# The late count read within the next uses, and the selection, ranks, masks and statistics of a neighbour-maximum kernel put at other uses

## The reference

```python
h = jnp.maximum(_layernorm(x, axis=-1), 0.0)
mask = A != 0                                   # A is adj
scores = jnp.where(mask, -jnp.arange(N), -inf)
vals, idx = jax.lax.top_k(scores, 25)           # the first 25 neighbours
feats = where(valid, h[idx], -inf); agg = feats.max(axis=2)
agg = jnp.where(degree <= 25, jnp.maximum(agg, 0.0), agg)
out = relu(concat([h, agg]) @ W + b)
return x + out
```

## Time and profile before

| what | us |
|---|---|
| median of 3 runs | 750.21 (750.12 to 751.39) |
| profiled execution | 756.99 |
| its span on the core | 755.3 |
| PE busy | 607.5 |
| DVE busy | 612.1 |
| ACT busy | 425.0 |
| POOL busy | 49.6 |
| mean granted TensorE clock | 0.966 of full |

### The profile page before, as it was taken

The page is one execution under the profiler, slowest core; times in us unless marked ns, Lnnn a source line. Parts: engine busy times, 40 slices in busy tenths (PEclk is TensorE's granted clock), DMA queues, the critical chain, the costliest instruction groups (busy, mean ns, idle before and its releaser), DMA issues.

```text
span 755.3 us, 9644 instructions
## 1 busy us (share of the span) xinstructions
PE 607.5 (80%) x2689; PEld 243.3 (32%) x2720; DVE 612.1 (81%) x813; ACT 425.0 (56%) x579; POOL 49.6 (7%) x38
## 2 busy tenths in 40 slices
PE   0555499888989799888889798898888699897975
PEld 0111133333333333334333333343333333342322
DVE  6111398987989789897989788997989498998986
ACT  0366374866367482686568483767569373746210
POOL 3000000300003000110003000210002000210000
PEclk9997699999999999999999989999999899999999
DMA  9584443547544663538744563548544662230100
GB/s 302 191 250 158 122 162 85 213 124 245 161 167 146 144 248 77 187 140 236 214 160 151 136 249 90 192 144 269 167 174 146 200 220 54 88 122 29 56 15 14
DMA packets 107877, 117.94 MB, mean 156 GB/s; under 512 B 74435, under 2 KB 94150, under 8 KB 103366
## 3 DMA queue, kind: packets, MB, share of 16 engines
q1 hardware_dynamic: 107846, 117.61, 49.1%
HBM read 58.85 MB, written 20.97 MB: 106 GB/s over the span
## 4 chain that ended last, share of the span: by engine, by line
PE 34%; DVE 24%; issue 15%; ACT 11%; SPq 10%; DMA 5%; DVEq 1%; ACTq 0%; another core or an unknown queue 0%
PE picked L556 10%; DVE best L729 9%; PE picked L557 9%; DVE late_hot L735 5%; PE ring L505 4%; SPq L239 4%; ACT late_rank L401 3%; DVE hot L710 3%; PE side L517 3%; SPq L241 3%; PE side L516 3%; SPq L263 3%; DMA mask_t<-mask 3%; DVE best L828 3%; ACT late L413 2%
## 5 line engine op out<-in xcount | busy, mean ns | idle before, releaser
L729 DVE TENSOR_TENSOR best<-picked,best 128x1024 f32<-128x1024 f32 x224 | 268.2, 1217 | 43.4 <-PE picked L557 42.3
L556 PE MATMUL picked<-hot,h_hi 128*128 128x512 f16 x512 | 201.4, 393 | 42.4 <-DVE best L729 28.9
L557 PE MATMUL picked<-hot,h_lo 128*128 128x512 f16 x512 | 199.9, 390 | 0.0
L408 ACT ACTIVATE chosen<-side,bias_cut 128x512 bf16<-128x512 f32 x128 | 88.0, 687 | 117.5 <-PE side L517 107.0
L556 PE MATMUL picked<-late_hot,hi_skew 128*128 128x512 f16 x336 | 127.6, 380 | 12.5 <-DVE late_hot L735 8.5
L557 PE MATMUL picked<-late_hot,lo_skew 128*128 128x512 f16 x336 | 127.3, 379 | 0.0
L828 DVE TENSOR_TENSOR best<-picked,best 128x1024 f32<-128x1024 f32 x84 | 102.6, 1221 | 8.2 <-PE picked L557 8.2
L401 ACT ACTIVATE late_rank<-ring,late_bias 128x512 bf16<-128x512 f32 x128 | 81.7, 688 | 44.3 <-PE ring L505 40.9
L710 DVE TENSOR_SCALAR hot<-rank 128x4096 f16<-128x4096 bf16 x64 | 83.3, 1303 | 26.7 <-ACT rank L401 26.7
L556 PEld LDWEIGHTS picked<-hot,h_hi 128*128 128x128 f16 x512 | 50.9, 99 | 153.5 <-DVE best L729 73.5
L437 ACT COPY best<-picked 128x1024 f32<-128x1024 f32 x32 | 32.3, 1014 | 113.5 <-PE picked L557 113.5
(11 more groups left out here) (72 smaller groups left out, 381.2 us busy)
## 6 DMA issues: line engine op xcount, KB each, us to landing
adj_in<-in_adj_dram SPq DMA_DIRECT2D x15, 2048.0 KB, 7.9
kept<-chosen SPq DMA_DIRECT2D x128, 128.0 KB, 1.8
picks<-kept SPq DMA_DIRECT2D x16, 1024.0 KB, 4.7
late_skew<-late SPq DMA_DIRECT2D x32, 192.0 KB, 2.3
x_in<-in_x_dram SPq DMA_DIRECT2D x8, 512.0 KB, 8.5
xres<-in_x_dram SPq DMA_DIRECT2D x16, 256.0 KB, 7.8
late_skew<-late SPq DMA_DIRECT2D x16, 256.0 KB, 2.4
late_skew<-late SPq DMA_DIRECT2D x32, 128.0 KB, 2.1
```

The costliest lines, as they stand in the source:

```text
L408: nc.scalar.activation(chosen[:, k, :], side[:, :], ACT.Sign, bias=bias_cut[:, 0:1], scale=-1.0).then_inc(chosen_made, 1)
L556: nc.tensor.matmul(dst, hi[:, slot, k, :], onehot, start=start, stop=False)
L557: return nc.tensor.matmul(dst, lo[:, slot, k, :], onehot, start=False, stop=stop)
L729: nc.vector.tensor_tensor(best[:, half, s, :, :], picked[s][:, :, :], best[:, half, s, :, :], ALU.max).then_inc(picked_read, 1)
```

## The change

- DVE: `count_rounds` moves from the end of a step (after `finish_group`) into the next step, behind the take of use 4 (COUNT_USE).
- PE and ACT: of the 8 late ranks 6 (LATE_EARLY) stay at a step's end, late ranks 6 and 7 move to use 4 of the next step (LATE_REST_USE). Late rank 3 on PE comes behind pick 3 instead of ahead of it. Ring positions are renumbered.
- Selection at uses 6 to 13 instead of 4 to 11, ranks at 5 to 11 instead of 4 to 11 (two at use 5); within a use the rank comes first.
- ACT: the four mask quarters at uses 5, 8, 10, 12 instead of after the uses; the waits for the transposes of the masks before and for adj stand ahead of the first quarter. find_late in one piece after the uses instead of at 12 and 14.
- Statistics at uses 13 and 14 and moments at 15 of the even step instead of 4, 5, 6 of the odd one; the spread at the even step's end; the gain at use 5 instead of 8.
- SP: the load of adj for g + 4 at a step's start; xres for g + 2 at its end.
- PE keeps the number that it waits for in a register (`known_due`).

```diff
-    SELECT_WITH, RANK_WITH = spread_over(4, 11), spread_over(4, 11)
-    FLAG_USES, RELU_USE, LATE_HOT_USES = (12, 14), 13, (7, 9)
-    STATS_USES, MOMENTS_USE, SPREAD_USE, GAIN_USE = (4, 5), 6, 7, 8
+    SELECT_WITH, RANK_WITH = spread_over(6, 13), spread_over(5, 11)
+    LATE_EARLY, LATE_REST_USE, COUNT_USE, LATE_HOT_USES = 6, 4, 4, (7, 9)
+    MASK_USES, RELU_USE = (5, 8, 10, 12), 13
+    STATS_USES, MOMENTS_USE, GAIN_USE = (13, 14), 15, 5
...
-    RANK_AT, LATE_AT = 0, K
+    FIRST_RING = K + LATE_EARLY
+    REST_AT, RANK_AT, LATE_AT = -LATE_EARLY, K - LATE_EARLY, 2 * K - LATE_EARLY
```

On SP, in a step:

```diff
-                if not at_end(it, u, 1):
-                    sp.wait_ge(result_made, g + 1)
-                    load_xres(g + 1, (u + 1) % 2)
+                if not at_end(it, u, 4):
+                    load_adj(g + 4, u % 2)
...
                 sp.wait_ge(stored[u % 2], 16 * (it * (UNROLL // 2) + u // 2 + 1))
-                if not at_end(it, u, 4):
-                    load_adj(g + 4, u % 2)
+                if not at_end(it, u, 2):
+                    load_xres(g + 2, u % 2)
```

On ACT:

```diff
                 for use in range(PAIRS, USES):
+                    if use == LATE_REST_USE:
+                        for k in range(LATE_EARLY, K):
+                            stage(at + REST_AT, k, late_rank, late_bias[:, k:k + 1])
+                    for k in RANK_WITH[use] if more else []:
+                        stage(at + RANK_AT, k, rank[:, (u + 1) % 2], late_bias[:, 0:1])
                     for k in SELECT_WITH[use] if not at_end(it, u, 2) else []:
                         choose(g + 2, k)
-                    for k in RANK_WITH[use] if more else []:
-                        stage(at + RANK_AT, k, rank[:, (u + 1) % 2], late_bias[:, 0:1])
-                    if use == SPREAD_USE and new_batch:
-                        spreads(batch)
+                    if use in MASK_USES and not at_end(it, u, 3):
+                        make_masks((u + 1) % 2, [MASK_USES.index(use)])
                     if use == RELU_USE and new_batch:
                         relu_parts(batch, slot)
-                    if use in FLAG_USES and more:
-                        for p in range(2):
-                            p += 2 * FLAG_USES.index(use)
-                            find_late(p, (u + 1) % 2, at + RANK_AT + 2 * p + 2)
+                if more:
+                    for p in range(PAIRS):
+                        find_late(p, (u + 1) % 2, at + RANK_AT + 2 * p + 2)
                 if new_batch:
                     turned_h(batch, slot)
-                if not at_end(it, u, 3):
-                    make_masks((u + 1) % 2)
+                if u % PER_BATCH == 0 and not at_end(it, u, PER_BATCH):
+                    spreads(batch_of(it, u) + 1)
...
-                    for k in range(K):
+                    for k in range(LATE_EARLY):
                         stage(at + LATE_AT, k, late_rank, late_bias[:, k:k + 1])
```

On PE:

```diff
                     pick_pair(g, use, slot)
+                    if use == LATE_REST_USE:
+                        for k in range(LATE_EARLY, K):
+                            late_ranks(g, at + REST_AT, k)
+                    for k in RANK_WITH[use] if more else []:
+                        ranks(g + 1, at + RANK_AT, k)
                     for k in SELECT_WITH[use] if not at_end(it, u, 2) else []:
                         place(g + 2, k, (CHAINS + 1) * g + 1)
-                    for k in RANK_WITH[use] if more else []:
-                        ranks(g + 1, at + RANK_AT, k)
...
                     late_ranks(g + 1, at + LATE_AT, 2)
+                    pick_pair(g + 1, 3, next_slot)
                     late_ranks(g + 1, at + LATE_AT, 3)
-                    pick_pair(g + 1, 3, next_slot)
                 project(g, it, u, new_batch)
                 if more:
-                    for k in range(HALF, K):
+                    for k in range(4, LATE_EARLY):
                         late_ranks(g + 1, at + LATE_AT, k)
```

On DVE:

```diff
                     take_pair(g, use, s)
                     if use == 5:
                         make_hot(BASE, s)
+                    if use == COUNT_USE:
+                        count_rounds(g, s)
                     if use in LATE_HOT_USES:
-                        dve.wait_ge(ring_read, at)
+                        dve.wait_ge(ring_read, at + REST_AT + K)
                         make_late_hot(LATE_HOT_USES.index(use), numbers[:, 1:2])
-                    if use in STATS_USES and new_batch:
+                    if use in STATS_USES and ahead:
...
                 finish_group(g, s, 16 * (it * (UNROLL // 2) + u // 2 + 1))
-                if more:
-                    count_rounds(g + 1, 1 - s)
```

More of the change, by code:

```diff
@@ L220, in ring_of @@
         def ring_of(it, u):
-            return (it * UNROLL + u + 1) * RING
+            return (it * UNROLL + u) * RING + FIRST_RING
         @block.sync
@@ L393, in make_masks @@
                 act.wait_ge(adj_loaded[slot], adj_due[slot])
-                for q in range(Q):
+            def make_masks(slot, quarters):
+                if 0 in quarters:
+                    await_masks(slot)
+                for q in quarters:
                     counts = adj_in[:, slot, q * N:(q + 1) * N].bitcast(U32)
@@ L445, in _ @@
                 choose(0, k)
-            make_masks(1)
+            make_masks(1, range(Q))
             turned_h(0, 0)
@@ L449, in _ @@
             for k in range(K):
-                stage(RANK_AT, k, rank[:, 0], late_bias[:, 0:1])
+                stage(0, k, rank[:, 0], late_bias[:, 0:1])
             find_late(0, 0, K)
@@ L457, in _ @@
                 choose(1, k)
[L458 to L460 removed]
+            for k in range(LATE_EARLY):
+                stage(K, k, late_rank, late_bias[:, k:k + 1])
+            make_masks(0, range(Q))
             def step(it, u):
@@ L600, in _ @@
             for k in range(K):
-                ranks(0, RANK_AT, k)
+                ranks(0, 0, k)
             pe.wait_ge(lo_made, 1)
@@ L607, in _ @@
                 place(1, k, None)
-            for k in range(K):
-                late_ranks(0, LATE_AT, k)
+            for k in range(LATE_EARLY):
+                late_ranks(0, K, k)
             pe.wait_ge(chosen_made, 2 * K)
@@ L800, in step @@
                 batch = batch_of(it, u + 1)
+                ahead = u % PER_BATCH == 0 and not at_end(it, u, PER_BATCH)
                 for use in range(PAIRS, USES):
@@ L806, in step @@
                         make_hot(BASE, s)
+                    if use == COUNT_USE:
+                        count_rounds(g, s)
                     if use in LATE_HOT_USES:
-                        dve.wait_ge(ring_read, at)
+                        dve.wait_ge(ring_read, at + REST_AT + K)
                         make_late_hot(LATE_HOT_USES.index(use), numbers[:, 1:2])
-                    if use in STATS_USES and new_batch:
+                    if use in STATS_USES and ahead:
                         half = STATS_USES.index(use)
-                        stats_of(batch, range(half * HALF, (half + 1) * HALF))
-                    if use == MOMENTS_USE and new_batch:
-                        moments_of(batch)
+                        stats_of(batch_of(it, u) + 1, range(half * HALF, (half + 1) * HALF))
+                    if use == MOMENTS_USE and ahead:
+                        moments_of(batch_of(it, u) + 1)
                     if use == GAIN_USE and new_batch:
```

9 lines of the change are left out of this document (6 added, 3 removed).

## The result

The change makes the kernel slower: **767.97 us** median of four runs (765.04 to 769.08) against 750.80 of four runs of the kernel before beside it (750.12 to 754.99), a ratio of **1.0211, interval 1.0163 to 1.0258**.

The account below looks back on a forecast made before the run. DVE (81%) and PE (80%) were taken as nearly full, leaving DVE's idle time and longer instructions; step changes, tails of -2.2 and clock +3 summed to +16.8 us on 756.99, scaled to 750.2 + 16.6 = 767, range 742 to 777.

Parts of the forecast that it names:

- Part 1: Count at use 4: 2.2 us less in 15 tails, count's 1.52 now in the front, true gain 0.7 a step.
- Part 2: Statistics a step sooner: some 2.1 us leave odd fronts and enter even ones, sum zero for a full DVE.
- Part 3: Gain at use 5: late_hot of use 7 waits for POOL's second instruction, 2.6 us; 1.2 more, 0.9 on the path.
- Part 4: ACT's new order: odd fronts +2.85 us, masks land 5.3 behind take 4, even front 24.95; the dear one.
- the six takes named: DVE's takes 7, 8, 9, 11, 12, 13 in even fronts, stalling on ACT's pace, together 4.1 us.
- Masks in time: Faster rival: masks land before 4.6 us behind take 4, even fronts 22.5, odd 21.7, total 730, halfway 740; chance 0.25.
- Part 5: PE's idle of 2.5 us in even fronts lowers its clock: 1.0 us in steps 2, 6, 10, each between 0 and 2.2.

Follow-up runs that it names:

- both_gain_late: Changed kernel with SP's mask transposes ahead of h's skew, all ACT mask quarters behind the uses, and the gain at use 9: 736.03 us, 0.9776.
- count_swap: flags_after with SP issuing the mask transposes ahead of the skew of h: 734.81 us, 0.9756.
- gain_late: Changed kernel with the gain at use 9 instead of 5: 758.09 us, 1.0077.
- count_and_uses: Changed kernel's count and later selection and ranks, with statistics, gain, find_late and masks as in the kernel before: 751.10 us, 0.9973.
- flags_after: count_and_uses with all find_late behind the uses, as in the change: 747.90 us, 0.9911.
- count_swap_sel: count_swap with selection at uses 5 to 12 and ranks at 4 to 11, each shifted one use sooner: 726.04 us, 0.9652.
- masks_first: Changed kernel with SP issuing the four mask transposes ahead of the skews of h: 756.48 us, 1.0058.
- quarters_after: Changed kernel with all four ACT mask quarters back behind the uses: 755.08 us, 1.0040.

## Why the prediction was right, and where it was off

The forecast was 767 us, with a range of 742 to 777 and slower at 0.70; the result is 768. The sign, the mechanism and its place were right. The last microsecond is partly luck: the predicted sum of 16.8 us was made against an execution that stood 6 us high, whereas between the second profile of before and the profile of after the span grew by 13.1 (and the profiled execution of after stands 2.9 us under its median). By its parts:

**Part 1, the count.** Right. DVE's idle before take 4 is 1.31 us in most steps (1.35 predicted) and 2.71 and 2.39 before those of steps 4 and 8, the first behind the loop's end. The count waits for nothing but 0.69 and 1.32 us within it in the same two steps, and the first take 4 of step 1 comes 2.8 us sooner (2.5). What gives the tail back is the rest.

**Part 2, statistics.** Right at zero, as far as the runs can tell: both_gain_late (736.0) and count_swap (734.8) differ in where statistics, the spread and the gain (use 9 or 8) stand, and their ranges overlap. The statistics by themselves were not tried.

**Part 3, POOL's port.** Right: late_hot stood until the second POOL instruction had ended. DVE and POOL, step 5 of after:

```profile
315.02 2.31 DVE L747 TENSOR_SCALAR late_hot<-late_rank,numbers 128x2048 f16<-128x2048 bf16 x1
...
328.39 3.01 DVE L722 TENSOR_SCALAR hot<-rank 128x4096 f16<-128x4096 bf16 x1
```

```profile
314.88 1.90 POOL L369 TENSOR_TENSOR h<-h,gain 128x1024 f32<-128x1024 f32 x1
...
328.19 2.13 POOL L358 TENSOR_TENSOR h_lo<-h,h_hi 128x1024 f16<-128x1024 f32 x1 [11.41 <-ACT h L428]
```

2.31 us against 2.6 predicted, as POOL's second instruction took 1.90 us and not 2.22; the odd front is 24.0 for 24.2. gain_late shows that this meeting is on the path.

There is a second meeting, of hot 1 with low_part, which got longer too: 3.01 us against 2.01 before. It makes DVE busier but hardly moves the front. PE's eighth late matmul and the late take that waits for it, the same step:

```profile
331.07 0.38 PE L563 MATMUL picked<-late_hot,lo_skew 128*128 128x512 f16 x1
...
331.49 1.23 DVE L842 TENSOR_TENSOR best<-picked,best 128x1024 f32<-128x1024 f32 x1
```

Two chains start at the last relu's end, 327.06 + 1.06 = 328.12. On PE turn_h and eight late matmuls end at 331.45, 3.33 us later. On POOL and DVE low_part and hot 1 end at 331.40, 3.28 later. The late take comes behind both. Which of the two is needed, count_and_uses tells: there hot 1 meets nothing and takes 1.22 us, and the eighth matmul still ends 3.29 us behind the relu (491.89 + 1.06 = 492.95, then 496.24), with DVE idle before the take. So the 3.27 us that the prediction took from the trace and its reason, PE's turn_h and late matmuls, were both right, and without the second meeting the front of after would be 0.1 us shorter at most. In flags_after, count_swap and count_swap_sel too PE's eighth late matmul ends at most 0.2 us behind hot 1 or with it. What sets their odd fronts is when the relus end, and so when choose 7 starts.

**Part 4, ACT's order.** Right, and the larger part. In step 6 place 0 stands at 5.6 us behind take 4 (5.3 predicted), PE idle 2.61 there (2.5), SP's first skew at 24.8 us of step 5 (25.0), even front of step 6 24.58 (24.95), its stalls at the six takes named: 0.76, 0.55, 0.28, 0.61, 0.29, 0.75, where 0.7, 0.8, 0.4, 0.9, 0.4, 0.9 stood. masks_first and quarters_after show each cause by itself. With the masks in time the even front was 22.53, the 22.5 of the rival *Masks in time*. The rest of that rival was too good: in masks_first, where its condition holds, the odd fronts were 23.97 and not its 21.7, and the time 756 us and not its 730. Mis-sized were steps 11 and 12: step 12 was to take 0.6 us more and took 3.6 less; step 11 grew by 4.3 (2.9 predicted), as its take 2 stood idle 3.66 us, PE waiting 3.03 of them for the late skew. The clock fell behind that wait (0.52 granted from 594.2 to 597.7) and not in step 12's front, as before (0.86 before, 1.00 after). Wait and fall both moved ahead of the step that had paid for them. The two together: +3.5 predicted, +0.7 measured.

**Part 5, the clock.** Mis-sized and misplaced. I set falls in steps 2, 6 and 10 at 1.0 us each, and counted those of before's steps 4 and 8 as standing. In the profile of after the clock stayed at 1.00 in the fronts of steps 6 and 10, behind 2.61 and 2.76 us without PE work, and fell in that of step 2, behind 2.71, and in those of steps 4 and 8: 0.93 of 25 to 26 us, so 1.2 GHz for 3.5 us. In before's first profile 0.85 of 23 us is 7 us at that level; a fall of that length cost 2.4 us, above the upper bound of 2.2. Accordingly steps 6 and 10 grew by 2.9 and 3.1 us (4.6 predicted with the clock) and steps 4 and 8, against a profile of before without falls, by 2.0 and 2.8 (0.1 and 0.5 predicted). The errors cancel within 1 us.

Between them the runs split the change's +2.1%, in ratio points of some 7.5 us each: 1.5 off with the masks in time, 1.7 off with the quarters behind the uses, 1.3 off with the later gain, and 4.4 off with all three (1.0211 to 0.9776). What remains open is why the clock falls in one step or execution and not in another at nearly equal idle; no run separates that.

## What to carry to other kernels

When a wait is as long as it is because of what a queue issues ahead, change that order before moving work to live with the lateness. Here putting four transposes ahead of fourteen small DMAs took 1.8% off, while the consumers' later place, once that was done, cost 12.5 us. Before an ACT instruction goes between two links of a chain, count who waits for the next link. After every move lay DVE's and POOL's instructions side by side, and then ask of each that got longer what else ends at the same moment: late_hot's 1.56 us beside POOL cost 1.35 a step, hot 1's 1.8 us cost at most 0.1, because PE ended as late. And profile the old kernel twice before a sum is made against its steps.

## What the runs showed of the hardware

**DVE and POOL take turns, by the whole instruction.** In the fourteen traces every hot (84 times) and every late_hot (84 times) that started while a POOL instruction of the batch's preparation ran ended a fixed time after POOL's end: 1.08 to 1.09 us for hot, 0.55 for late_hot. For hot: 328.39 + 3.01 = 331.40, POOL's end at 328.19 + 2.13 = 330.32, difference 1.08; in flags_after 324.32 and 323.23, 1.09. For late_hot: 317.33 and 316.78, 0.55; before, 320.08 and 319.53, 0.55. So a meeting lengthens the instruction by what is left of the other's: from 0.4 us (hot 1.66 for 1.22, count_swap_sel) to 1.8 (hot 3.01 for 1.22) here; whether the step gets longer by it is another matter. POOL is held as well: low_part took 2.28 us where it started 0.93 us into a hot (count_and_uses), against 2.13 in after, and the second instruction of `normalize` took 2.22 us in before, where it was issued while late_hot still stood, against 1.90 in after. The Trainium skill (SBUF — State Buffer, "SBUF: two separate sides") calls the port pair an exclusive lock for a whole instruction; these rows agree with it. The f32 maxima, by contrast, ran at 1.20 to 1.23 us each beside POOL's instructions.

**The same program, the same idle, another clock.** Steps 4 and 8 of before: 0.85 in one execution, 1.00 in the next, 2.4 us each. That is most of the 5.2 us by which the two profiles differ, and per step it is more than several of the effects above. In the kernel after PE's idle before place 0 was 2.71, 2.61 and 2.76 us in steps 2, 6 and 10, and the granted clock of the fronts 0.93, 1.00 and 1.00.
